# The quantised layer's end computed by batches of 256 tokens, and two of its softmax steps on GpSimd

## What is computed

```python
x_norm = fq(layernorm(x, g1, beta1), s_n1)
qkv = fq(x_norm @ fq(w_qkv).T + b_qkv, s_qkv)            # 12 heads of 16
attn = int_softmax(fq(q @ k.T / 4, s_attn), s_attn)      # 256 x 256 a batch and head
x_attn = fq((attn @ v) @ fq(w_proj).T + b_proj, s_sv)
x = fq(x + x_attn, s_r1)
x_norm = fq(layernorm(x, g2, beta2), s_n2)
h = fq(gelu(x_norm @ fq(w_fc1).T + b_fc1), s_act)        # 768 wide
h = fq(h @ fq(w_fc2).T + b_fc2, s_m2)
x = fq(x + h, s_r2)                                      # added to the stream
```

## Time and profile before

| | us |
|---|---|
| median of three runs (1108.31 to 1113.07) | 1109.13 |
| the profiled execution, own time | 1103.81 |
| its span | 1102.0 |
| VectorE busy in the span | 812.6 (74%) |
| PE busy | 854.1 (78%) |
| ScalarE busy | 601.2 (55%) |
| Pool busy | 340.8 (31%) |
| quantised layer, first load to last sum | 380.7 to 636.4 |

### The profile page before, as it was taken

The page is one execution under the profiler, slowest core; times in us unless marked ns, Lnnn a source line. Parts: engine busy times, 40 slices in busy tenths (PEclk is TensorE's granted clock), DMA queues, the critical chain, the costliest instruction groups (busy, mean ns, idle before and its releaser), DMA issues. The chain is left out here.

```text
span 1102.0 us, 17488 instructions
## 1 busy us (share of the span) xinstructions
PE 854.1 (78%) x6037; PEld 577.9 (52%) x6037; DVE 812.6 (74%) x1738; ACT 601.2 (55%) x1012; POOL 340.8 (31%) x335
## 2 busy tenths in 40 slices
PE   8779999985989656667772455899999938668991
PEld 3333333333579622223352244799888825557991
DVE  6589999994674389999957875688888557583763
ACT  2755454421466467889971353577776227255760
POOL 0016666644056312222200006122222430024335
PEclk8889999997999865555556768899999969969995
DMA  8086666603000000000000073599996447102653
GB/s 263 34 214 169 167 168 160 153 19 86 1 1 2 20 1 0 1 1 1 1 1 0 1 211 107 149 266 258 263 260 178 133 121 199 53 23 88 210 204 89
DMA packets 61591, 117.78 MB, mean 107 GB/s; under 512 B 10240, under 2 KB 37312, under 8 KB 61504
## 3 DMA queue, kind: packets, MB, share of 16 engines
q1 hardware_dynamic: 58432, 110.38, 36.6%
q0 software_dynamic: 3072, 6.30, 1.9%
HBM read 90.99 MB, written 16.81 MB: 98 GB/s over the span
## 5 line engine op out<-in xcount | busy, mean ns | idle before, releaser
L459 POOL TENSOR_TENSOR hC<-hs,Cb 128x1024 f32<-128x1024 f32 x47 | 110.9, 2359 | 125.0 <-DVE hs L498 125.0
L498 DVE TENSOR_TENSOR_SCAN hs<-ps_l,dBu 128x1024 f32<-128x1024 f32 x48 | 110.0, 2291 | 2.8 <-ACT ps_l L590 1.2
L658 PE MATMUL ps_l<-hC,selT 128*96 128x512 f32 x192 | 93.2, 609 | 1.5 <-POOL hC L459 1.5
L590 ACT ACTIVATE ps_l<-d_sp,Am 128x1020 f32<-128x1020 f32 x48 | 53.5, 1115 | 71.5 <-DVE hs L498 71.3
L643 PE MATMUL ps_l<-du,sel 96*128 96x512 f32 x192 | 90.5, 593 | 1.4 <-DVE dBu L491 1.4
L1905 POOL CAST m_h_hi<-m_h 128x512 f16<-128x512 f32 x54 | 49.1, 910 | 136.6 <-DVE m_h L1982 136.6
L1993 DVE TENSOR_TENSOR m_h_lo<-m_h,m_h_hi 128x512 f16<-128x512 f32 x62 | 42.8, 692 | 35.3 <-POOL m_h_hi L1905 33.3
L2311 PE MATMUL ps_m<-m_wd_hi,m_h_hi 128*128 128x192 f16 x248 | 63.1, 255 | 6.4 <-issue 3.6
L1213 POOL TENSOR_SCALAR q_e<-q_qi 128x512 int16<-128x512 f16 x48 | 30.0, 625 | 119.1 <-ACT q_qi L1480 60.5
L1585 PE MATMUL ps_l<-q_xi,identh 128*128 128x512 f16 x48 | 28.6, 595 | 49.0 <-DVE q_ex L1340 28.1
L2198 ACT ACTIVATE m_act<-ps_m 128x512 f32<-128x512 f32 x62 | 36.8, 593 | 51.8 <-PE ps_m L2293 51.6
(11 more groups left out here) (548 smaller groups left out, 2799.8 us busy)
## 6 DMA issues: line engine op xcount, KB each, us to landing
d_sp<-scan_d SPq DMA_DIRECT2D x48, 512.0 KB, 4.6
m_sta<-in_m_ua SPq DMA_DIRECT2D x25, 512.0 KB, 4.3
m_stb<-in_m_ub SPq DMA_DIRECT2D x50, 256.0 KB, 5.8
m_std<-in_m_dn SPq DMA_DIRECT2D x25, 384.0 KB, 6.7
gw_dn_in<-gw_dn SPq DMA_DIRECT2D x10, 576.0 KB, 3.3
scratch_x<-zero SPq DMA_DIRECT2D x1, 4416.0 KB, 20.5
m_xg<-scratch_x SPq DMA_DIRECT2D x23, 192.0 KB, 6.5
scratch_y<-m_o SPq DMA_DIRECT2D x23, 192.0 KB, 6.5
```

Of the source, the lines that this page charges most:

```text
L459: pool.tensor_tensor(hC[:, n % 2, :], hs[:, n % 2, :], Cb[:, which(n), :], ALU.mult).then_inc(weighted, 1)
L498: v.tensor_tensor_scan(hs[:, n % 2, ::step], dA(n)[:, ::step], dBu[:, n % 2, ::step], 0.0, ALU.mult, ALU.add).then_inc(scanned, 1)
L590: act.activation(dst[:, :, o:o + L - 1], d_sp[:, n % NSP, :].rearrange("p (b t) -> p b t", t=L)[:, :, o:o + L - 1], ACT.Exp, scale=Am[:, c ...
L658: mm = pe.matmul(ps[0:DI, 6 + half, :], selT[:, n % NG, :], hC[:, n % 2, half * BANK:(half + 1) * BANK], start=(n == STEPS), stop=(m == ST ...
```

## The change

- The clip of `lt` (in `start`) and the quotient go to Pool, with the first half of the six late `operand` steps (`clip_operand`). Pool's queue per head is now `clip(h+1)`, `quotient(h)`, `q_e` of h.
- A batch's sums are turned, copied, projected and read in the loop, some 15 steps after its heads (`TURN = 25`): `turn_sums`, `copy_turned`, `project_sums`, `read_projection`, all in bank 7. Pool requantises batches 0 and 1 in three parts in steps 29 to 31 and 41 to 43, batch 2 behind its heads; VectorE does batch 3.
- The second norm is in pieces of 4, 2 and 2 tiles; gain and shift are columns, applied by ScalarE out of the turned f32 tiles (`recentre`); round and clip follow (`clip_norm`).
- The up products go by half of the tokens; Gelu, rounding, a clip to f16 `hh` and the last pass are interleaved. The bias of the second product is a product of a row of ones with `brow`. ScalarE reads the down products by batch and rounds the stream; `ACT.Gelu` has a first use of one column ahead of the Gelus.
- The later layers' `use` of the shared LayerNorm is one less, `q_rows` has three rows and `q_cols` four columns.

```diff
@@ Pool @@
+                def clip(h):
+                    pool.wait_ge(shifted, h + 1)
+                    both = lt[:, h % 2, :, :].rearrange("p q k -> p (q k)")
+                    pool.tensor_scalar(both, both, CENTRE + 127.0, CENTRE - 128.0, ALU.min, ALU.max).then_inc(clipped, 1)
+                def quotient(h):
+                    pool.wait_ge(diff, (h + 1) * QT)
+                    if h >= 2:
+                        pool.wait_ge(rest, h - 1)
+                    pool.tensor_scalar(qi[:, h % 2, :], xi[:, h % 2, :, :].rearrange("p q k -> p (q k)"), kf[:, K_INV:K_INV + 1],
+                                       kf[:, K_QB:K_QB + 1], ALU.mult, ALU.add).then_inc(quot, 1)
...
                 for h in range(HEADS):
+                    if h + 1 < HEADS:
+                        clip(h + 1)
+                    if 1 <= h < 7:
+                        clip_operand(5 + h)
+                    quotient(h)
                     pool.wait_ge(quot, h + 1)
...
+                    if h >= TURN + 4 and h < TURN + 4 + 2 * NH and (h - TURN - 4) % NH < 3:
+                        b, part = divmod(h - TURN - 4, NH)
+                        requantise(6 * b, b, part)
+                        if part == 2:
+                            restore(b)
@@ VectorE @@
                 def start(h):
-                    v.wait_ge(shifted, h + 1)
-                    v.tensor_scalar(lt[:, h % 2, :, :], lt[:, h % 2, :, :], CENTRE + 127.0, CENTRE - 128.0, ALU.min,
-                                    ALU.max).then_inc(clipped, 1)
                     v.wait_ge(clipped, h + 1)
...
+                    if n in (TURN + 3, TURN + 3 + NH, TURN + 5 + 2 * NH):
+                        read_projection((n - TURN - 3) // NH)
+                    if n == HEADS + 2:
+                        statistics(0)
+                    if n == HEADS + 4:
+                        normalise(0)
+                    if n == STEPS - 1:
+                        statistics(1)
+                normalise(1)
+                clip_norm(4)
+                clip_norm(5)
...
+                read_projection(3)
+                v.wait_ge(proj_read, 4)
+                requantise(3, S_SV, S_R1)
+                statistics(2)
+                normalise(2)
...
+                for n in range(FF2 + 2):
+                    if n < FF2:
+                        v.wait_ge(gelu, n + 1)
+                        v.tensor_scalar(hf[:, n % 4, :], hf[:, n % 4, :], r(S_ACT), MAGIC, ALU.mult, ALU.add).then_inc(h_round, 1)
+                    if 1 <= n <= FF2:
+                        clipped_up(n - 1)
+                    if n >= 2:
+                        whole(n - 2)
+                    if n == 3:
+                        clip_norm(6)
+                        clip_norm(7)
...
+                for p in range(NB + 1):
+                    if p < NB:
+                        add_down(p)
+                    if p >= 1:
+                        add_stream(p - 1)
@@ PE @@
+                    if n in (TURN, TURN + NH, TURN + 2 * NH):
+                        turn_sums((n - TURN) // NH)
+                    if n in (TURN + 2, TURN + 2 + NH, TURN + 2 + 2 * NH):
+                        project_sums((n - TURN - 2) // NH)
+                    if n == HEADS + 8:
+                        turn_norm(0, 4)
+                turn_sums(NB - 1)
+                turn_norm(4, 6)
+                project_sums(NB - 1)
...
+                for n in range(4):
+                    up_product(n)
+                turn_norm(6, 8)
+                for n in range(4, FF2 - 2):
+                    up_product(n)
+                for p in range(2):
+                    down_product(p)
+                    up_product(FF2 - 2 + p)
+                for p in (2, 3):
+                    down_product(p)
```

More of the change, by code:

```diff
@@ L1208, in _ @@
                     take(0, group)
+                pool.wait_ge(constants, 1)
+                clip(0)
                 for h in range(HEADS):
+                    if h + 1 < HEADS:
[3 more added lines that the diff above has]
+                    quotient(h)
                     pool.wait_ge(quot, h + 1)
@@ new lines, in normalise, with read_projection @@
+                def normalise(g):
+                    lo, hi = LN2[g]
+                    v.wait_ge(std, g + 3)
+                    step(v.reciprocal(rs[:, 0, lo:hi], sd[:, lo:hi]))
+                    for t in range(lo, hi):
+                        v.tensor_scalar(N[:, t, :], U[:, t, :], mv[:, t, 0:1], rs[:, 0, t:t + 1], ALU.subtract, ALU.mult).then_inc(normed, 1)
+                def read_projection(b):
+                    v.wait_ge(o_proj, b + 1)
+                    v.scalar_tensor_tensor(pj[:, b, :].rearrange("p (t c) -> p t c", c=C),
+                                           ps[:, 7, 0:QT * C].rearrange("p (t c) -> p t c", c=C), k(K_PROJ),
+                                           rows[:, 1, :].unsqueeze(1).broadcast_to([P, QT, C]), ALU.mult, ALU.add).then_inc(proj_read, 1)
@@ L1510, in _ @@
-                for n in range(FT * NHALF):
-                    act.wait_ge(up, n + 1)
-                    act.wait_ge(hq, max(n - 3, 0))
-                    act.activation(hf[:, n % 4, :], ps[:, n % 4, :], ACT.Gelu, scale=kf[:, K_FC1:K_FC1 + 1],
-                                   bias=b1[:, n // 2:n // 2 + 1]).then_inc(gelu, 1)
+                    if n in (TURN + 1, TURN + 1 + NH, TURN + 1 + 2 * NH):
+                        copy_turned((n - TURN - 1) // NH)
+                    if n == HEADS + 3:
+                        roots(0)
@@ new lines, in _ @@
+                roots(1)
+                act.wait_ge(scaled2, 1)
+                recentre(4)
+                recentre(5)
+                take_sums(NB - 1)
+                copy_turned(NB - 1)
+                roots(2)
+                act.activation(warm[:, :], kf[:, K_CENTRE:K_CENTRE + 1], ACT.Gelu)
+                for n in range(FF2):
+                    act.wait_ge(up, n + 1)
+                    if n >= 4:
+                        act.wait_ge(h_clip, n - 3)
+                    act.activation(hf[:, n % 4, :], ps[:, RING[n % 4], :], ACT.Gelu, scale=kf[:, K_FC1:K_FC1 + 1],
+                                   bias=b1[:, n % FT:n % FT + 1]).then_inc(gelu, 1)
+                    if n == 1:
+                        recentre(6)
+                        recentre(7)
@@ L1516, in _ @@
+                for p in range(NB):
+                    act.wait_ge(down, p + 1)
+                    act.activation(pj[:, p, :], ps[:, (4, 7, 2, 3)[p], 0:QT * C], ACT.Identity, scale=kf[:, K_FC2:K_FC2 + 1],
+                                   bias=kf[:, K_ZERO:K_ZERO + 1]).then_inc(down_read, 1)
+                    if p >= 1:
+                        round_stream(p - 1)
+                round_stream(NB - 1)
             @block.tensor
```

308 lines of the change are left out of this document (186 added, 122 removed).

## The result

The changed kernel takes 1104.65 us (median of 12, 1099.16 to 1111.21), the kernel before beside it 1112.70: ratio 0.9938, 95% interval 0.9915 to 0.9960. A second round gave 0.9933 (0.9908 to 0.9958). It is faster by 0.6%, 7 us, where 1.7% was forecast; 1104.65 lies 0.65 us above the range, and the bulk of the gain is missing.

A forecast was written before the change was run, and what follows sets the result against it. VectorE was taken to bound the heads, and the end to be a chain with little side by side. Heads +0.6, loads -0.6, drain +5 and end -24 gave -19 us from 1109.1: 1090 us, range 1074 to 1104.

The forecast's parts named there:

- The end, -24: From W, the end of the last weighing, to the layer's last sum: 43.8 us instead of 67.7, ends -16 and -30.
- an end over 52: Sign that the forecast was wrong: over 52 us from the last weighing to the last sum, about 44 expected.
- a down product of 2.4 us: In the end on PE: two tiles of 0.74 and a 0.48 bias product, keeping back steps 10 and 11 by about 1.5 each.
- the nearer end, -16: Smallest gain the forecast allowed from the last weighing to the last sum: 16 us; the far bound was -30.
- The heads, +0.6: The layer's 48 heads: -1.4 plain, -4 heads 12 to 19, -1.5 first 12, +5, +1 and +1.5 for added work.
- the term -1.4: 27 plain steps of the last 28 heads: 2.65 us each, saved clip comes back as blocking; ends -8.6 and +8.
- Batch work: Added in the heads: Pool's requantisation +5, PE's f32 transposes and products +1, VectorE's reads and last sum +1.5.
- The drain, +5: Weighing and summing after the heads: added PE turns and projection and VectorE norm cost 5 us, ends +2 and +8.
- the loads, -0.6: The layer's loads: rows shrink from five to three, cutting VectorE's 2.08 us wait by 0.6.
- Rival (4): Batches do not overlap in the end; drain grows by 8, dense steps stretch to 1.1 us: 1104; chance 8%.
- Rival (2): In the heads blocking costs more than the clip: 3.0 us for a plain head, 1102 in all; chance 12%.
- Rival (3): Pool bounds the heads: clip and quotient take 1.24 us each, not 0.62, giving 1119; chance 7%.

The follow-up runs named there:

- e1: Changed kernel without its eight ones-by-bias products, the last dense product's bias left out; ratio to the kernel before 0.9890, end 46.2 us.
- e4: Kernel before with only the heads' clip and quotient moved to Pool; ratio to the kernel before 0.9977, heads 148.5 us.
- e5: Changed kernel with the last sum's copy, turn, projection and read ahead of the norm's second piece; ratio to the kernel before 0.9899, end 50.3 us.
- e2: Changed kernel with up products 10 and 11 ahead of all down products; ratio to the kernel before 0.9857, end 49.6 us.
- e6: Changed kernel with up products 10 and 11 first and the bias as one bf16 product of 96 rows; ratio to the kernel before 0.9877, end 42.4 us.
- e9: Changed kernel with quotient on ScalarE, up products first, 96-row bf16 bias prepared in the drain, last sum first; ratio to the kernel before 0.9868.
- e13: Changed kernel with quotient on ScalarE, ups first, 96-row bf16 bias prepared between dense steps 1 and 2, last sum first; ratio to before 0.9830, 1089.51 us.
- e14: Changed kernel with quotient on ScalarE, ups first, 96-row bf16 bias prepared between dense steps 1 and 2, last sum not earlier; ratio to before 0.9848.

## Why the prediction was wrong

In the layer -19 us were forecast and -8.7 came (255.7 to 247.0). By its own terms:

- **The end, -24: the step that failed.** It came to -14.4, W + 53.3 and not 43.8; "an end over 52" was one of its signs of being wrong. Of the 9.5 us, 2.1 come before the dense steps: steps 4 to 11 start at W + 23.6 and not 21.5, since the statistics wait for Pool's requantisation of batch 2, done at W + 2.9 and forgotten in the sum, and the projection took 2.87. Then the last step ends at W + 40.1 and not 32.6 (5.4 more), and the rest takes 13.2 and not 11.2 (2.0), since PE and not VectorE sets it. Both go back to one term: a down product of 2.4 us (two tiles, each 0.74 and a bias product of 0.48) that keeps back steps 10 and 11 by about 1.5 each. A down product measured 3.85, and the steps were kept back by 4.0 and 3.8 (the brackets 4.04 and 3.84 above). Of that, 1.45 each is the price. Another 1.0 each was left out whatever the price: the up product itself, which stands in PE's queue behind the down product (608.52 to 609.51). In e1, whose first down product took 1.9 us, less than the 2.4 of the forecast, step 10 was still kept back by 2.06:
```profile
606.16 0.49 DVE L1531 TENSOR_SCALAR q_hf<-q_hf,q_rc 128x512 f32<-128x512 f32 x1 [2.06 <-ACT q_hf L1660]
```
Both prices came from rows at a mixed clock: the stretches of the projection and of the down products in the kernel before, and then the changed kernel's first and last down products:
```profile
575.00:582.80 7.80, 7.72 (x32) 7.42 (x32) 1.85 (x3) 0.00 (x0) 0.00 (x0) 0.70 0.00 0
620.30:626.30 6.00, 5.90 (x48) 5.47 (x48) 3.15 (x7) 0.00 (x0) 0.00 (x0) 0.69 0.00 0
```
```profile
604.70:608.50 3.80, 3.80 (x16) 2.54 (x17) 1.69 (x6) 0.39 (x1) 0.00 (x0) 0.50 0.00 0
617.10:625.10 8.00, 7.99 (x32) 4.92 (x32) 6.28 (x15) 1.97 (x3) 0.00 (x0) 0.50 0.00 0
```
There the clock was 0.70 and 0.69, here 0.50: 1.0 us for the bias, 1.14 for the six products. For the six the clock is nearly the whole difference: 1.07 from start to start, and 0.74 x 0.69/0.50 = 1.02. For the bias it is not: at 0.50 the changed kernel's own projection has four f32 products of 192 columns in 2.87 us, 0.72 each, while the bias, alone between bf16 products, held PE for 0.93 from start to start. The price was taken from a row of like products; why one alone costs more no run here tells. e1 took 7.1 us off the end with that one line. That the clock could stay at 0.50 through the whole stretch was in no bound, and the nearer end, -16, did not hold the -14.4.
- **The heads, +0.6: measured +3.6.** The clip and quotient were to bring -6.9 and brought -3.2 (e4). The mechanism held: a `q_xi` pair takes 0.90 in most plain heads where 0.60 was, and a plain head 2.69 us where 2.65 was forecast, so the term -1.4 measured -1.2. Off were the guesses for heads 12 to 19 (-4, measured -1.9) and for the first 12 (-1.5, measured -0.1). Batch work was forecast at +7.5 and came to 6.8, its shares otherwise: Pool 2.6 and not 5, PE 2.6 and not 1, reads and constants 1.6 (1.5 forecast). The quotient was 0.77, not 0.62, worth 1 us.
- **The drain, +5: measured +2.4**, within its ends; **the loads, -0.6: -0.3** in the first profiles and +0.1 in the second, so nothing.
- **The total.** Rival (4) named the time, 1104, with a stretched dense stage and the last batch behind foreign work in ScalarE's queue. The queue cost 3.0 (e5), but the stretch was PE's, not VectorE's steps (0.96 from one to the next, 0.94 forecast), and the drain did not grow by 8. The figure met by luck too: it is a gain of 5 us on a kernel before of 1109.1, and what came is 8 on one of 1112.7. Rival (2)'s 1102 was right in sign for the heads, but its plain head of 3.0 us was not seen. Rival (3) did not happen: Pool's 0.77 is far from 1.24.

## What to carry to other kernels

Price a new TensorE product at the slow of its two clocks unless the stretch it goes into shows the other, and where it will stand alone not from a row of its like. Then ask which engine sets that stretch once it is there, and count in its queue everything that stands ahead of the next result: here a bias row cost more than the order of two products. Between two engines that block each other a saving can come back as waiting: moving one small operation to Pool paid 5 us, none of it in a plain head, and moving a second gave 3 back. Before a chain is moved into idle time of one engine, look at what runs on its neighbour there.

## What was not expected of the hardware

PE at 16.10 busy of 16.10 us was granted 0.50 all along (e2), and with a f32 bias product of 64 rows or a bf16 one of 1 row the clock was 0.50 over all down products too. It reached 1.00 in e6, e9, e13 and e14 with a bf16 product of 96 rows, but in e13 and e14 before the first of these had run. A f32 product of 192 columns held PE for 0.93 us alone between bf16 products at 0.50, and for 0.72 in a row of four. On Pool a two-step scaling of 512 f16 elements took 0.62 us with constants and 0.77 with per-partition columns. Unchanged layers differed by up to 14 us between single profiles (466 to 480), while a stage of the changed layer came again within 0.5.
